# Row maxima of two quantized feed-forward layers: from a GpSimd all-reduce to transposes on TensorE, with both layers in one program per engine

## The reference

```
def _ste_quant_rows(a):
    scale = max(abs(a), axis=-1, keepdims=True) / 127.0
    scale = maximum(scale, 1e-08)
    return clip(round(a / scale), -127.0, 127.0) * scale

def _linear8bit(x, W, b):
    col_max = max(abs(x), axis=rows)
    outlier = col_max > 3.0
    x_in, x_out = where(outlier, 0.0, x), where(outlier, x, 0.0)
    y = _ste_quant_rows(x_in) @ _ste_quant_rows(W).T
    return y + x_out @ W.T + b

h = _linear8bit(layernorm(x), W1, b1)
return x + _linear8bit(h, W2, b2)
```

## Time and profile before

| | |
|---|---|
| median of 3 runs | 1022.08 us |
| lowest and highest of them | 1015.89 and 1022.70 us |
| the profiled execution | 1024.18 us |
| its span in the profile | 1022.4 us |
| busy share of PE, DVE, ACT, POOL | 89%, 72%, 60%, 42% |
| mean granted clock of PE | 0.943 of full |

### The profile page before, as it was taken

One profiled execution on the slowest core, in us unless ns is written; L12 is line 12 of the kernel. 1 busy time (PEld: TensorE's weight loads), 2 busy tenths in 40 slices (PEclk: granted clock), 3 DMA queues, 4 the chain that ended last, 5 costly groups with the idle time before them and its releaser, 6 DMA issues. The chain is left out here.

```text
span 1022.4 us, 18954 instructions
## 1 busy us (share of the span) xinstructions
PE 911.0 (89%) x6771; PEld 833.2 (81%) x6771; DVE 738.3 (72%) x1150; ACT 614.2 (60%) x1015; POOL 432.6 (42%) x274
## 2 busy tenths in 40 slices
PE   5999999899978899999898999957489999499987
PEld 5998888688857799889898889846389999498986
DVE  6547666644556387788787888868888889778954
ACT  4514434645516388878787788755467787366652
POOL 0210000244425856564464555302076676165663
PEclk9999999999988999999999999958789999699989
DMA  7567667666653788766676767824033442224221
GB/s 276 226 202 272 228 237 267 250 269 268 220 150 107 230 249 258 199 196 171 176 213 179 210 177 209 279 63 171 16 128 121 164 164 83 83 84 165 85 80 42
DMA packets 90215, 183.20 MB, mean 179 GB/s; under 512 B 9600, under 2 KB 67744, under 8 KB 87584
## 3 DMA queue, kind: packets, MB, share of 16 engines
q1 hardware_dynamic: 89664, 182.22, 54.3%
q10 hardware_dynamic: 480, 0.03, 0.0%
HBM read 161.51 MB, written 11.53 MB: 169 GB/s over the span
## 5 line engine op out<-in xcount | busy, mean ns | idle before, releaser
L52 PE MATMUL bank<-act_all,W_all 128*128 128x256 f32 (+1 forms) x512 | 158.6, 310 | 10.9 <-POOL W_all L1598 7.9
L52 PE MATMUL bank<-act_all,wh 128*128 128x256 f32 x512 | 146.3, 286 | 1.8 <-PEq L857 1.7
L54 PE MATMUL bank<-act_all,W_all 128*128 128x256 f32 (+1 forms) x512 | 146.3, 286 | 0.0
L53 PE MATMUL bank<-act_all,wh 128*128 128x256 f32 x512 | 146.1, 285 | 0.0
L54 PE MATMUL bank<-act_all,wl 128*128 128x256 f32 x512 | 146.0, 285 | 0.0
L1318 DVE TENSOR_TENSOR pl<-bank,ph 128x512 f16<-128x512 f32 x128 | 88.3, 690 | 56.1 <-ACT ph L1272 55.3
L459 POOL TENSOR_TENSOR xa_WT_l<-ring,xa_WT_h 128x1024 fp32r<-128x1024 f32 x16 | 41.5, 2610 | 186.3 <-ACT xa_WT_h L454 186.3
L850 POOL TENSOR_TENSOR wl<-ring,wh 128x1024 fp32r<-128x1024 f32 x32 | 76.5, 2391 | 102.2 <-ACT wh L842 102.1
L1261 ACT ACTIVATE bank<-bank,exp_shift 128x512 f32<-128x512 f32 x128 | 84.5, 660 | 47.5 <-PE bank L1189 46.6
L1598 POOL TENSOR_TENSOR W_all<-rnd,W_all 128x512 fp32r<-128x512 f32 x72 | 92.8, 1301 | 46.2 <-ACT W_all L1524 39.1
L52 PEld LDWEIGHTS bank<-act_all,W_all 128*128 128x128 f32 x512 | 100.2, 196 | 13.4 <-POOL W_all L1598 10.1
(11 more groups left out here) (219 smaller groups left out, 2625.3 us busy)
## 6 DMA issues: line engine op xcount, KB each, us to landing
ring<-in_ctx_dram SPq DMA_DIRECT2D x16, 2048.0 KB, 8.0
ring<-in_L_attn_Wq_rope_dram SPq DMA_DIRECT2D x32, 1024.0 KB, 7.9
ring<-in_L_ffn_W_dram SPq DMA_DIRECT2D x16, 2048.0 KB, 7.6
panel<-in_L_ffn_W_dram SPq DMA_DIRECT2D x48, 512.0 KB, 4.3
qmix<-qrope SPq DMA_DIRECT2D x128, 64.0 KB, 2.6
w1p<-in_L_ffn_W_dram SPq DMA_DIRECT2D x16, 512.0 KB, 3.9
ring<-in_L_xattn_Wq_dram SPq DMA_DIRECT2D x2, 2048.0 KB, 11.7
ring<-in_L_xattn_Wk_dram SPq DMA_DIRECT2D x2, 2048.0 KB, 8.1
```

Source lines behind the costliest of these rows:

```text
L52: pe.matmul(out, lh, rh, start=start, stop=False, skip_group_check=True)
L53: pe.matmul(out, lh, rl, start=False, stop=False, skip_group_check=True)
L54: return pe.matmul(out, ll, rh, start=False, stop=stop, skip_group_check=True)
```

## The change

The partition reduction moves from POOL to PE. PE transposes the two 128x128 halves of the row-maximum tile, so that the 256 rows lie on partitions (`turn_rowmax`). DVE reduces that to one number per row, and makes the step and the inverse from 128x2 numbers (`row_factors`). PE transposes these back, each read with a step of zero so that every partition gets them (`spread_factors`), and DVE and ACT copy the inverse and the step out of PSUM (`copy_inverse`, `copy_factor`).

```
+            def turn_rowmax(pe, src):
+                for t in range(QT):
+                    last = pe.transpose(bank[4][:, t * P:(t + 1) * P], src[:, t * P:(t + 1) * P], ident[:, :])
+                last.then_inc(row_turned, 1)
+            def row_factors(dve, link, n):
+                dve.wait_ge(row_turned, n + 1)
+                link(dve.tensor_reduce(rowc[:, 0, :], bank[4][:, 0:T].rearrange("p (t k) -> p t k", t=QT), axis=AX.X, op=ALU.max))
+                link(dve.tensor_scalar(rowc[:, 1, :], rowc[:, 0, :], 1.0 / QMAX, TINY_SCALE, ALU.mult, ALU.max))
+                dve.reciprocal(rowc[:, 2, :], rowc[:, 1, :]).then_inc(row_factor, 1)
+            def spread_factors(pe, n):
+                pe.wait_ge(row_factor, n + 1)
+                for i, out in enumerate((bank[4][:, T:2 * T], bank[5][:, 0:T])):
+                    for t in range(QT):
+                        last = pe.transpose(out[:, t * P:(t + 1) * P], rowc[:, 1 + i, t:t + 1].to_broadcast([P, P]), ident[:, :])
+                last.then_inc(row_spread, 1)
+            def copy_inverse(dve, link, n):
+                dve.wait_ge(row_spread, n + 1)
+                link(dve.tensor_copy(rsx[:, :], bank[5][:, 0:T]))
+            def copy_factor(act, n, dst):
+                act.wait_ge(row_spread, n + 1)
+                act.activation(dst[:, :], bank[4][:, T:2 * T], ACT.Copy).then_inc(sx_copied, 1)
```

In the first layer the order on PE, ACT, POOL and DVE changes with it:

```
 PE
                     transpose_rows(pe, onat, 2, y3_ready, base=4, free=lambda: pe.wait_ge(x2_done, 2 * QT))
-                    for k in range(4, KT - 1):
-                        turn(0, 0, k)
+                    pe.wait_ge(y_max, KT)
+                    pe.wait_ge(y3_out, KT // 2)
+                    turn_rowmax(pe, rowmax)
+                    turn(0, 0, 4)
+                    spread_factors(pe, 0)
+                    turn(0, 0, 5)
+                    pe.wait_ge(sx_copied, 1)
                     first_step()
 PE, in first_step
-                            if k == 0:
-                                turn(0, 0, KT - 1)
-                            elif k >= 2:
+                            if k < 2:
+                                turn(0, 0, KT - 2 + k)
+                            else:
 ACT: the four Abs copies (line 1563) before the four plain copies (line 1564), not in turn; then
+                    copy_factor(act, 0, sx1)
                     high_y(0)
 POOL
-                    pool.wait_ge(y_max, KT)
-                    pool.partition_all_reduce(allmax[:, :], rowmax[:, :], P, RMAX).then_inc(rm1, 1)
 ...
-                    pool.wait_ge(r_max, NF + 1)
-                    pool.partition_all_reduce(allmax[:, :], runmax[:, :], P, RMAX).then_inc(par, 1)
+                    ffn2_gpsimd(pool)
 DVE
-            EARLY = 3
+            EARLY = 2
-                    for k in range(EARLY):
+                    rounded(0, 0, mag1)
+                    row_factors(dve, link, 0)
+                    for k in range(1, EARLY):
                         rounded(0, k, mag1)
-                    dve.wait_ge(rm1, 1)
-                    link(dve.tensor_scalar(sx1[:, :], allmax[:, :], 1.0 / QMAX, TINY_SCALE, ALU.mult, ALU.max))
-                    link(dve.reciprocal(rsx[:, :], sx1[:, :]))
+                    copy_inverse(dve, link, 0)
 DVE, the last step
-            TILES_AT_LAST = ((), (0,), (), (), (1,), (), (), (2, 3))
-            MAXIMA_AT_LAST = ((), (0,), (1, 2), (3,))
+            TILES_AT_LAST = ((), (0,), (), (), (1,), (), (2,), (3,))
+            MAXIMA_AT_LAST = ((), (0,), (1,), (2, 3))
```

The second block is gone. Its programs are the same but for their starts, and each engine calls its own behind its first-layer program, without a meeting:

```
+            def ffn2_tensor(pe):
+                pe.sem_inc(j_done, KT)
+                pe.sem_inc(j_ready, KT)
+                pe.wait_ge(h_scaled, CH + NF)
+                for a in (6, 7):
+                    clear(a)
+                pe.wait_ge(r_max, NF + 1)
+                turn_rowmax(pe, runmax)
+                spread_factors(pe, 1)
+                pe.wait_ge(sx_copied, 2)
+                clear(4)
+                pe.wait_ge(q2_chain, 3)
+                clear(5)
+                pe.wait_ge(b_ready, 4 + (NW1 + 1) * KT)
+                pe.wait_ge(b_lo, 4 + (NW1 + 1) * KT)
+                pe.wait_ge(t_ready, (NW1 + 2) * CH)
+            def ffn2_scalar(act):
+                copy_factor(act, 1, sx2)
+            def ffn2_vector(dve):
+                row_factors(dve, link, 1)
+                copy_inverse(dve, link, 1)
+                dve.wait_ge(b_lo, 4 + (NW1 + 1) * KT)
```

More of the change, by code:

```diff
@@ new lines, in build, with ffn2_sync @@
+            yo = oT
+            NCH = 2 * NQ
+            def ffn2_sync(sp):
+                with sp.Fori(0, NQ - 1) as i:
+                    for b in range(2):
+                        sp.wait_ge(j_ready, i * (2 * KT) + KT * (b + 1))
+                        load(sp, b, raw(b), w2_t[:, CH * b:CH * b + CH, ds(i * D + D, D)])
+                for t in range(QT):
+                    sp.wait_ge(y_out, QT + t + 1)
+                    sp.dma_start(out_t[:, t, :], xr[:, t, :]).then_inc(out_done, 16)
+                sp.wait_ge(out_done, QT * 16)
@@ new lines, in ffn2_scalar, with scale_rows, high, high_h @@
+            def ffn2_scalar(act):
+                def scale_rows(c1, b, n, j):
+                    if j == 0:
+                        landed(act, b, n)
+                    act.activation(raw(b)[:, j, :], raw(b)[:, j, :], ACT.Copy,
+                                   scale=rw2[:, CH * b + j:CH * b + j + 1]).then_inc(t2_ready, 1)
+                def high(c1, k):
+                    act.wait_ge(j_rnd, c1 * KT + (4 + k + 1))
+                    act.wait_ge(j_done, c1 * KT + (k + 1))
+                    act.activation(V_h[:, k, :], rnd[k % 4][:, :], ACT.Copy).then_inc(j_hi, 1)
+                def high_h(nq, k):
+                    n = nq * KT + k
+                    act.wait_ge(q2_b, n + 1)
+                    act.activation(hq_h[:, ds(n, 1), :].rearrange("p a q -> p (a q)"),
+                                   hT[:, ds(n, 1), :].rearrange("p a q -> p (a q)"), ACT.Copy).then_inc(q2_hi, 1)
+                act.sem_inc(t2_ready, 2 * CH)
+                act.sem_inc(j_hi, KT)
+                copy_factor(act, 1, sx2)
+                for k in range(KT):
+                    high_h(0, k)
+                def step(c, b, n1, nq, more, first=False):
+                    for k in range(KT):
+                        for j in SCALE2_AT[k] if n1 is not None and not first else ():
+                            scale_rows(c + 1, 1 - b, n1, j)
+                        if k < KT - LAG:
+                            if not first:
+                                high(c, k + LAG)
+                        elif n1 is not None:
+                            high(c + 1, k + LAG - KT)
+                        if more:
+                            high_h(nq + 1, k)
+                step(0, 0, USE_W2, 0, True, first=True)
+                step(1, 1, USE_W2 + 1, 0, False)
+                with act.Fori(1, NQ - 1) as i:
+                    for b in range(2):
+                        step(i * 2 + b, b, i + (USE_W2 + b), i, b == 0)
+                step(NCH - 2, 0, USE_W2 + NQ - 1, None, False)
+                step(NCH - 1, 1, None, None, False)
+                for r in range(KT):
+                    act.wait_ge(y_chain, r + 1)
+                    act.activation(yo[:, r, :], yo[:, r, :], ACT.Identity, bias=b2c[:, r:r + 1]).then_inc(y_bias, 1)
```

319 lines of the change are left out of this document (133 added, 186 removed).

## The result

The changed kernel takes 1008.83 us (median of 20 runs, 1000.4 to 1013.87), the kernel before 1016.37 us (median of 20, 1007.7 to 1023.0). The ratio is 0.9924 with a 95% interval of 0.9901 to 0.9946, a gain of 7.7 us (5.5 to 10.1). Timed again in a later comparison it was 0.9910 (0.9876 to 0.9944). The forecast was 5.5 us of gain and 1016.5 us.

What follows compares the result with a forecast made beforehand. PE sets the pace in both layers, with holes at two hand-overs. Gains of 4.1 us (second: 3.5 + 0.6) and 1.4 us (first) sum to 5.5 us, from 1022.08 to 1016.5 us; range 1010 to 1023.

Steps and rivals of the forecast that it cites:

- the level: Whole kernel: median of three runs before the change, 1022.08 us, from which the 5.5 us gain was subtracted.
- the earlier maximum: Between the layers: new tables end the last running maximum at 875.4 us, a gain of 0.6 us (0 to 1.5).
- The chain at the second hand-over: Between the layers: four links from last maximum to first scaled tile take 3.5 us (2.6 to 5.0) for 7.02.
- the walk: Last step before the second layer: order followed, one POOL collision left, putting the last maximum at 875.4 us.
- The meeting: Between the layers: all engines met, ending together with the all-reduce; its loss was to gain nothing of its own.
- The first hand-over: Before the first layer: without POOL's reduction PE starts 2.4 us earlier, of which 1.4 us stays (-2.4 to 2.4).
- the middle between two reckonings: First hand-over: 1.4 us taken between a gain of 2.0 from summed parts and 0.7 from walking the order.
- DVE's way: First layer's start: DVE's 17.54 us from first scaling to later roundings decides how much of PE's earlier start stays.
- The port rival: First hand-over: DVE waits out every POOL subtraction it meets, losing 2.4 us; time 1020.4 us, chance 0.14.
- The clock: Rival, between the layers: PE's clock holds or comes back sooner, giving 1013.2 us; chance 0.12.
- Late code: New chain: PE, ACT and DVE run into code not yet fetched, stalling; time 1026.6 us, chance 0.08.
- the rival on the slower side: The case of code not there in time in one straight program: 1026.6 us, far end 1031.6; chance 0.08.

Runs made afterwards that it cites:

- the repeat: The changed kernel run once more with no edit; ratio to the kernel before 0.9910, median 1006.75 us.
- the unused reduction: Changed kernel plus POOL's old all-reduce of rowmax before its first subtraction, its result read by nobody; one execution, 1013.12 us.
- the third tile: Changed kernel with EARLY 3 for 2: DVE rounds a third weight tile before copying the inverse; ratio to the kernel before 0.9944, median 1011.89 us.

## Why the prediction was off, point by point

The direction and the mechanism were right at both hand-overs; the level was wrong, and this alone put the number outside the range; in the sum of the gain one term was mis-sized, the earlier maximum.

- **The level** is the step that failed: "the median of the runs, which becomes 1022.08 - 5.5 = 1016.6". I set the range around the median of three runs, 1022.08 us, and took the spread of those three for the uncertainty of a difference. Twenty runs have their median at 1016.37, and 5.7 of the 7.7 us of the miss come from here. With the same effect on that level I would have said 1010.9 us.
- **The chain at the second hand-over.** Forecast 3.5 us for 7.02, measured 3.03 (3.28 with the turning transposes at the low clock, 2.56 with all of them at the high one). The reduction, the copy, and the spread read with a step of zero came out as the rows of ordinary ones had said: 0.42, 0.42, and 1.11 us.
- **The earlier maximum** is the term that was mis-sized: "I come to 875.4 us: a gain of 0.6 (0 to 1.5)". It was 1.86. The tables gave 0.97; the other 0.89 I put down to DVE's phase against PE in the steps ahead, which the walk took over unchanged from the trace of before. Worse than the size was the logic behind it: in the kernel before, this maximum was no bound. The reduction started 5.8 us after POOL's last subtraction, whenever the maximum came. The term counts only together with the move away from POOL. The sum was right by construction, the reading of "7.02 us from the last maximum" as one price was not.
- **"The meeting ended together with the all-reduce, so its loss gains nothing of its own."** Right for the old reduction (7.82 us without a meeting); with the transposes a meeting would cost 1.2 us.
- **The first hand-over.** Forecast 1.4 us, measured 1.56 (1.17 in the repeat). The middle between two reckonings came out, but PE's own start was too early in the forecast: about 7 us after the maxima, 2.4 earlier than before; measured 7.87, 1.7 earlier. It was released by DVE, as said. The cause, POOL's idle time behind its reduction, is shown by the unused reduction. What I made of DVE's way was half true, as the third tile shows. The port rival (1020.4 us) did not happen: the code instructions still took 2.67 us for two once and 1.71 once, beside POOL's subtractions, but the first two subtractions were done (at 724.29 us) before the first code instruction (725.37).
- **The clock.** I gave it 0.12 as an either-or, and priced the slow first products of the second layer at 2.6 us. The first products did run at 0.50 for a shorter time, 2.89 us instead of 6.12, and it bought nothing. The changed kernel waited for ACT's row scaling 23.17 us into the layer, and in both kernels PE's next two waits for that scaling end at the same time, 55.82 and 88.84 us into the layer before, 55.70 and 88.71 after. The 1.63 us that the second layer is shorter lie behind the third wait, which took 3.04 and 3.03 us and was followed by slow products both times. Windows from the end of this wait on (length, busy and count per engine, granted clock, DMA), first of the kernel before, then of the changed one:

```profile
974.02:980.00 5.98, 5.98 (x28) 5.98 (x29) 3.27 (x4) 2.43 (x5) 5.20 (x4) 0.50 0.40 166
```

```profile
953.72:957.00 3.28, 3.28 (x17) 3.28 (x18) 1.98 (x2) 2.05 (x4) 2.82 (x3) 0.55 0.75 307
957.00:960.00 3.00, 3.00 (x29) 3.00 (x28) 2.28 (x3) 0.64 (x1) 3.00 (x3) 1.00 0.00 0
```

  No edit of the change acts there. Of the five profiles with this program and a gap of about 9.4 us three have a second layer of 135.6 to 135.8 us and two one of 137.0 and 137.2. (In the run with the first reduction back most of the excess lies between the second and the third wait, which end 55.91 and 90.09 us into the layer.) So 1.6 of the 8.5 us are had in some executions, and about 6.9 us are the change's own. The five profiles with a gap of 10.6 us or more all have 136.9 to 137.2; whether a shorter gap makes the shorter layer likelier is not shown.
- **Late code** did not show: no wait in the new chain is down to "issue", and no packet of an instruction queue lies between 853 and 866 us, around the gap of the changed kernel. With that the rival on the slower side is out.
- **What I did not look for** was a bound inside the second layer. I let every microsecond of an earlier start count in full, and it does: from its first product the layer takes no longer than before. But a faster start, with fewer products at the low clock or with none, runs into ACT's row scaling 23 us on.

What stays open: where the 3 to 13 us between executions ahead of the first layer's maxima arise. Whole profiles show fewer or more windows at 0.50 to 0.91 between 300 and 700 us, but no run here was made to separate them. What POOL does in its idle times before and after the reduction is open too: that they are loads of its code is inferred from the length of the first kind, and in the kernel before no DMA packet lies between 734.5 and 741.5 us or between 873.5 and 879.3 us.

## What to carry to other kernels

A rare instruction on an engine has a price before and behind it that its own record does not show: 1.08 us were recorded, while the engine stood still for about 6 us ahead (where it had worked until then) and 7 us behind, and the second can hurt work that never reads the result. Price a removed instruction by the neighbours' waits on its engine, and ask of each end of a chain whether it really releases the next link. Before counting a faster stretch in full, look for the first place behind it where the gaining engine has to wait for a slower one; here two small moves in that engine's order were worth about 6 us behind the maxima, nearly as much as the whole change. And take the level from many runs, or forecast the difference and its range by themselves.

## What the runs showed of the hardware

- GpSimd: `PARTITION_ALL_REDUCE` started 5.82 and 5.98 us after the last ordinary instruction, and the next ordinary one came 7.04, 6.73 and 6.71 us after it. After 29 to 30 us of idle time it started 0.14 us behind the maximum that released it.
- A transpose whose stationary operand is read with a step of zero costs what an ordinary one costs: 1.11 us for four at the low clock, as the earlier trace rows.
- The granted clock fell 5.5 us after PE's last product in the changed kernel's profile and 4.4 us before, and came back after 2.9 and 6.1 us of products. With 30 clearing matmuls of zeros and six transposes in the gap of 9.02 us, PE busy for 7.99 of them, it did not fall.
- DVE's inverse takes 1.75 us on 128x256 and 0.17 us on 128x2.
